# Third pass over the edges of a four-layer graph network: gathered rows as three bf16 parts

## The chip, the cores and the metric

The kernel runs on one core of one Trainium2 chip. The metric is the device time of one execution in microseconds (us). The five engines are TensorE (PE; its weight loads are listed apart as PEld), VectorE (DVE), ScalarE (ACT), GpSimd (POOL) and SyncE (SP).

## What is computed

A graph of 6250 nodes with 128 features each and 200000 edges, sorted by destination, goes through four layers. The third is a plain graph convolution:

```python
h = relu(layernorm(x))
h = feat * (out_deg ** (-0.5))[:, None]
agg = jax.ops.segment_sum(h[src], dst, num_segments=n)   # fp32
rst = relu((agg @ weight) * (in_deg ** (-0.5))[:, None] + bias)
x = x + rst
```

The other three layers are attention layers over the same edges. All is fp32.

## The kernel before

Nodes stand in 49 tiles of 128. Edges stand in 391 groups of 512 (4 tiles of 128 edges); a group whose edges reach over a border of node tiles is visited once for each node tile, so there are 440 visits, in the order that the destinations give. Each layer is a phase that writes a table of rows to DRAM and a pass over the edges that gathers from it. The passes run one after another; every phase ends in a barrier of all engines.

In the third pass (`conv_pass`, 5771 to 8032 us of the span):

- GpSimd runs `fetch`: for each of 392 groups four indirect DMAs (L465, 1568 in all) bring 128 rows each of the table `conv_rows` into one of 14 slots. A row has 129 fp32 numbers, 516 B: 128 features and a 1, which counts the in-degree. Before it fills a slot again it waits (L463) until TensorE's visits of the group that was there are done (`sum_done`). In its other three passes `fetch` puts a small tensor operation (L472, the pause) behind each gather; in this pass it does not.
- VectorE makes, 8 visits ahead, the one-hots of a visit (`pick`, L1033): 4 matrices of 128 edges by 128 nodes, written as fp32.
- TensorE multiplies them with the gathered rows, 4 matmuls of 129 columns a visit that add into one of 8 PSUM banks (L1022). It reads slot and due group of four visits at a time from a table (L411, L386), and waits for the group's rows, the one-hots and the bank. The trace shows each fp32 matmul as two weight loads and two matmuls.
- VectorE adds the bank to the node tile's sums in SBUF (L1042), after the add before it is done.

The loops are rolled: 32 visits are written out, then 16 visits an iteration. ScalarE has no work in this pass.

In the phase ahead (`conv_inputs`, l2pre, 5608 to 5771 us) ScalarE writes the finished rows (L1825) in 7 sets of 7 node tiles into two buffers, and SyncE stores each set to DRAM (L1741). GpSimd works on the set's inputs (L1753 to L1758), clears the sums (L1761) and has nothing after.

## Time and profile before

| | us |
|---|---|
| median of 3 runs | 10693.53 (10691.29 to 10695.21) |
| profiled execution, its own time | 10696.8 |
| its span, first to last instruction | 10695.1 |
| gathers of pass 1, first to last issue | 535.7 to 2938.3 |
| pass 2 | 3116.2 to 5567.7 |
| pass 3 | 5776.9 to 8021.0 |
| pass 4 | 8184.6 to 10578.7 |

A row of a group of instructions gives line, engine, operation, output and inputs, the count, then busy time, mean ns of one, and the idle time of the engine just before them by what ended it. Where a wait's releaser is inferred, "issue" means that the profile shows nothing that the engine waited for. A timeline row gives start, duration and, in brackets, the idle time before.

### The profile page before, as it was taken

Reading aid. Unit: us, or ns where it says so; the run is one execution under the profiler, and the core shown is the slowest. Engines: PE = TensorE matmul, PEld = TensorE weight load, DVE = VectorE, ACT = ScalarE, POOL = GpSimd, SP = SyncE. Lnnn points to the kernel's source line nnn. Section 1 sums busy time; section 2 is a strip of 40 time slices with the busy share of each in tenths; the row PEclk is TensorE's granted clock in tenths of the full one; section 3 lists DMA queues with packets and bytes.
Section 4 is the critical chain, followed back from the end, with each engine's and each line's share of the span. In section 5 each row is a group of like instructions: output and inputs, shape, how many; then the busy total and the mean of one; then the engine's idle time right before and its main releaser. Section 6 shows DMA issues by size and latency. Waiting matters only on the chain. (4 is left out here: it accounts for less than half of the span.)

```text
span 10695.1 us, 165052 instructions
## 1 busy us (share of the span) xinstructions
PE 6694.1 (63%) x38290; PEld 5319.6 (50%) x38291; DVE 5218.1 (49%) x13802; ACT 2509.1 (23%) x6808; POOL 7984.3 (75%) x11114
## 2 busy tenths in 40 slices
PE   4977777777756667666663333333337777777776
PEld 3656665655535555555553232232224555555554
DVE  4266666666665555555553111111114555555555
ACT  1333333333343333333333000000002111111111
POOL 0188888888848888888865666666663888888884
PEclk9966666676765555555556555565556666666667
DMA  3333333333312212222111222222222332333332
GB/s 112 148 88 88 87 87 87 87 88 88 87 46 47 46 44 46 45 46 45 44 40 46 46 46 46 47 46 46 46 46 63 87 87 87 87 87 87 87 87 63
DMA packets 379652, 731.26 MB, mean 68 GB/s; under 512 B 169770, under 2 KB 219233, under 8 KB 373126
## 3 DMA queue, kind: packets, MB, share of 16 engines
q0 software_dynamic: 251264, 621.88, 22.1%
q1 hardware_dynamic: 100762, 97.56, 2.8%
q10 hardware_dynamic: 27500, 10.39, 0.4%
q8 instruction: 48, 0.79, 0.0%
q14 instruction: 78, 0.64, 0.0%
HBM read 652.50 MB, written 76.88 MB: 68 GB/s over the span
## 5 line engine op out<-in xcount | busy, mean ns | idle before, releaser
L465 POOL DMA_INDIRECT edges_rows<-conv_rows,edges_idx_r x1568 | 1536.9, 980 | 773.6 <-issue 457.9
L465 POOL DMA_INDIRECT edges_rows<-gat_rows,edges_idx_r x1568 | 1562.8, 997 | 336.1 <-issue 260.1
L465 POOL DMA_INDIRECT edges_rows<-kv_typed,edges_idx_r x1568 | 1597.6, 1019 | 267.6 <-issue 263.5
L465 POOL DMA_INDIRECT edges_rows<-kv_rows,edges_idx_r x1568 | 1522.2, 971 | 271.6 <-issue 267.7
L1022 PE MATMUL edges_ps_sum<-edges_rows,edges_pick 128*128 x3520 | 763.3, 355 | 1511.7 <-issue 1386.9
L629 PE MATMUL edges_ps_sum<-edges_wv,edges_pick 128*128 128x132 f32 x7040 | 1671.9, 409 | 20.9 <-issue 13.4
L472 POOL TENSOR_TENSOR edges_pause<-edges_pause 128x56 f32<-128x56 f32 x4704 | 1599.9, 340 | 108.1 <-issue 18.1
L629 PEld LDWEIGHTS edges_ps_sum<-edges_wv,edges_pick 128*128 128x128 f32 x7040 | 1427.0, 297 | 256.6 <-issue 246.5
L1022 PEld LDWEIGHTS edges_ps_sum<-edges_rows,edges_pick 128*128 128x128 f32 x3520 | 647.9, 257 | 1627.1 <-issue 1625.7
L1120 PE MATMUL edges_ps_q<-q,edges_pick_t 128*128 x3520 | 748.7, 379 | 674.5 <-DVE edges_prod L1184 649.7
L1042 DVE TENSOR_TENSOR sums<-sums,edges_ps_sum 128x129 f32 x440 | 126.9, 288 | 1858.5 <-DMA edges_rows<-gat_rows,edges_idx_r 1486.5
L1120 PEld LDWEIGHTS edges_ps_q<-q,edges_pick_t 128*128 128x128 f32 x3520 | 645.4, 274 | 779.2 <-issue 779.0
L1110 PE MATMUL edges_ps_sum<-edges_wv,edges_pick 128*128 128x136 f32 x3520 | 814.0, 400 | 7.4 <-DVE sums L1206 7.4
L1110 PEld LDWEIGHTS edges_ps_sum<-edges_wv,edges_pick 128*128 128x128 f32 x3520 | 697.6, 286 | 166.1 <-issue 161.3
L611 PE MATMUL edges_ps_q<-q,edges_pick_t 128*128 x3520 | 750.1, 378 | 36.7 <-issue 15.2
L611 PEld LDWEIGHTS edges_ps_q<-q,edges_pick_t 128*128 128x128 f32 x3520 | 655.9, 277 | 66.5 <-issue 60.3
L815 DVE TENSOR_TENSOR edges_wv<-edges_rows,edges_wv 128x512 f32<-128x512 f32 x880 | 636.0, 723 | 3.8 <-issue 3.0
L1151 ACT ACTIVATE edges_wv<-edges_gap 128x32 f32<-128x32 f32 x440 | 113.1, 257 | 2075.7 <-DVE edges_gap L1213 1857.8
L1184 DVE TENSOR_TENSOR edges_prod<-edges_rows,edges_ps_q 128x512 f32<-128x512 f32 x440 | 301.5, 685 | 585.1 <-POOLq L475 306.5
L915 DVE TENSOR_TENSOR edges_lo_hot<-iota_bf,edges_src_lo 128x512 bf16<-128x512 bf16 x440 | 314.3, 714 | 558.7 <-remote 425.7
L1174 DVE TENSOR_TENSOR edges_pick<-edges_ps_iota,edges_local 128x512 f32<-128x512 f32 x440 | 304.3, 692 | 543.1 <-issue 530.0
L772 DVE TENSOR_TENSOR x<-iota_bf,edges_local 128x512 bf16<-128x512 bf16 x440 | 314.8, 715 | 473.4 <-issue 385.4
(345 smaller groups left out, 10934.8 us busy)
## 6 DMA issues: line engine op xcount, KB each, us to landing
kv_typed<-l0pre_out SPq DMA_DIRECT2D x49, 1024.0 KB
edges_rows<-kv_typed,edges_idx_r POOLq DMA_INDIRECT x1568
edges_rows<-gat_rows,edges_idx_r POOLq DMA_INDIRECT x1568
edges_rows<-conv_rows,edges_idx_r POOLq DMA_INDIRECT x1568
edges_rows<-kv_rows,edges_idx_r POOLq DMA_INDIRECT x1568
edges_feat_r<-visit_features ACTq DMA_DIRECT2D x660, 10.0 KB
kv_rows<-l3pre_kv SPq DMA_DIRECT2D x7, 896.0 KB
edges_flag_r<-visit_flags ACTq DMA_DIRECT2D x220, 16.0 KB
```

Of the source, the lines that this page charges most:

```text
L465: pool.indirect_dma_start(rows[:, k, g * width:(g + 1) * width], None, table, bass.IndirectOffsetOnAxis(ap=idx_r[:, k, g:g + 1], axis=0)). ...
L472: nc.gpsimd.tensor_tensor(pause, pause, pause, ALU.add).then_inc(paused, 1)
L611: mm = nc.tensor.matmul(ps_q[s % 2][:, g * D:(g + 1) * D], pick_t[:, s % 2, g * P:(g + 1) * P], q[:, bass.ds(b * D, D)], start=True, stop= ...
L629: mm = nc.tensor.matmul(ps_sum[s % 2][:, 0:aw], pick[:, s % 2, g * P:(g + 1) * P], wv[:, s % 3, g, :], start=g == 0, stop=g == G - 1)
L772: nc.vector.tensor_tensor(pick_b[:, s, :].rearrange("p (g n) -> p g n", g=G), c["iota_bf"].unsqueeze(1).broadcast_to([P, G, P]), bcast(loc ...
L815: nc.vector.tensor_tensor(wv4[:, s % 3, :, :, 0:hd], vals, bcast(wv4[:, s % 3, :, :, hd], [P, G, heads, hd]), ALU.mult).then_inc(wv_done, 1)
L915: ins = nc.vector.tensor_tensor(hot[:, s % 2], c["iota_bf"][:, 0:n].unsqueeze(1).broadcast_to([P, G, n]), bcast(digits[:, bass.ds(u * G, G ...
L1022: mm = nc.tensor.matmul(ps_sum[k % banks][:, 0:aw], pick[:, k % deep, g * P:(g + 1) * P], now[:, g, :], start=g == 0, stop=g == G - 1)
L1110: mm = nc.tensor.matmul(ps_sum[s % 2][:, 0:aw], pick[:, s % 6, g * P:(g + 1) * P], wv[:, s % 3, g, :], start=g == 0, stop=g == G - 1)
L1120: mm = nc.tensor.matmul(ps_q[s % 2][:, g * D:(g + 1) * D], pick_t[:, s % 2, g * P:(g + 1) * P], q[:, bass.ds(b * D, D)], start=True, stop= ...
L1174: nc.vector.tensor_tensor(pick[:, s % 6, :].rearrange("p (g n) -> p g n", g=G), ps_iota[:, 0:P].unsqueeze(1).broadcast_to([P, G, P]), bcas ...
L1184: nc.vector.tensor_tensor(prod[:].rearrange("p (g d) -> p g d", g=G), of_slot(rows, slot, width)[:, :, 0:D], ps_q[s % 2][:].rearrange("p ( ...
```

## The change

The table `conv_rows` holds for each feature three bf16 numbers whose sum is the fp32 number exactly: the high part, the high part of the rest, and what is left. A row is 385 bf16 numbers (770 B): 128 high, 128 mid, 128 low parts and the 1. GpSimd makes the parts in `conv_inputs`: four operations a set, each behind the one before by a semaphore. The one-hots are written as bf16, TensorE does one matmul of 385 columns a tile, and VectorE adds mid, low with the count, and high in three operations, each behind the one before.

```diff
+PARTS = 3 * D + 1
@@ conv_pass
-        rows = p.sb("rows", [P, SLOTS, G * aw])
+        rows = p.sb("rows", [P, SLOTS, G * PARTS], BF16)
-        pick, local = p.sb("pick", [P, deep, GE]), ...
+        pick, local = p.sb("pick", [P, deep, GE], BF16), ...
-                        mm = nc.tensor.matmul(ps_sum[k % banks][:, 0:aw], pick[:, k % deep, g * P:(g + 1) * P], now[:, g, :],
+                        mm = nc.tensor.matmul(ps_sum[k % banks][:, 0:PARTS], pick[:, k % deep, g * P:(g + 1) * P], now[:, g, :],
-                    nc.vector.tensor_tensor(blk, blk, ps_sum[k % banks][:, 0:aw], ALU.add).then_inc(acc_done, 1)
+                    nc.vector.tensor_tensor(blk[:, 0:D], blk[:, 0:D], ps_sum[k % banks][:, D:2 * D], ALU.add).then_inc(mid_done, 1)
+                    dve.wait_ge(mid_done, u + 1)
+                    nc.vector.tensor_tensor(blk, blk, ps_sum[k % banks][:, 2 * D:PARTS], ALU.add).then_inc(low_done, 1)
+                    dve.wait_ge(low_done, u + 1)
+                    nc.vector.tensor_tensor(blk[:, 0:D], blk[:, 0:D], ps_sum[k % banks][:, 0:D], ALU.add).then_inc(acc_done, 1)
@@ conv_inputs
-        table = p.sb("table", [P, 2, CH, D + 1])
+        table, rest_rows = p.sb("table", [P, 2, CH, D]), p.sb("rest_rows", [P, CH, D])
+        parts = p.sb("parts", [P, 2, CH, PARTS], BF16)
@@ SyncE
-                    sp.wait_ge(row_done, (k + 1) * CH)
-                    sp.dma_start(dram["conv"][...], table[:, k % 2]).then_inc(stored[k % 2], 16)
+                    sp.wait_ge(low_cut, k + 1)
+                    sp.dma_start(dram["conv"][...], parts[:, k % 2]).then_inc(stored[k % 2], 16)
@@ GpSimd
+                pool.wait_ge(framed, 1)
+                for k in range(SETS):
+                    row = table[:, k % 2]
+                    high, mid, low = (parts[:, k % 2, :, n * D:(n + 1) * D] for n in range(3))
+                    pool.wait_ge(row_done, (k + 1) * CH)
+                    if k >= 2:
+                        pool.wait_ge(stored[k % 2], 16 * (k // 2))
+                    if k:
+                        pool.wait_ge(low_cut, k)
+                    nc.gpsimd.tensor_copy(high, row).then_inc(high_cut, 1)
+                    pool.wait_ge(high_cut, k + 1)
+                    nc.gpsimd.tensor_tensor(rest_rows[:], row, high, ALU.subtract).then_inc(high_off, 1)
+                    pool.wait_ge(high_off, k + 1)
+                    nc.gpsimd.tensor_copy(mid, rest_rows[:]).then_inc(mid_cut, 1)
+                    pool.wait_ge(mid_cut, k + 1)
+                    nc.gpsimd.tensor_tensor(low, rest_rows[:], mid, ALU.subtract).then_inc(low_cut, 1)
@@ ScalarE
-                        act.wait_ge(stored[t // CH % 2], 16 * (t // CH // 2))
+                        act.wait_ge(low_cut, t // CH - 1)
@@ VectorE
-                nc.vector.memset(table[:], 1.0).then_inc(framed, 1)
+                nc.vector.memset(parts[:], 1.0).then_inc(framed, 1)
```

On VectorE a visit of the third pass reads as follows before the change (`edges_pick` are the one-hots, `sums` the node tiles' sums, TENSOR_LOAD the read of the node tile's number):

```order
L1042 TENSOR_TENSOR sums<-sums,edges_ps_sum 128x129
L1033 TENSOR_TENSOR edges_pick<-iota_bf,edges_local 128x512
L377 TENSOR_LOAD seat_rows
L1042 ISA
L1042 TENSOR_TENSOR sums<-sums,edges_ps_sum 128x129
```

and with it, where two adds more stand between two makings of one-hots:

```order
L1048 TENSOR_TENSOR sums<-sums,edges_ps_sum 128x128
L1035 TENSOR_TENSOR edges_pick<-iota_bf,edges_local 128x512
L378 TENSOR_LOAD seat_rows
L1044 ISA
L1044 TENSOR_TENSOR sums<-sums,edges_ps_sum 128x128
L1046 TENSOR_TENSOR sums<-sums,edges_ps_sum 128x129
L1048 TENSOR_TENSOR sums<-sums,edges_ps_sum 128x128
```

On TensorE the visit has the same instructions in the program, only the matmul's shape differs. Before:

```order
L1022 ISA
L1022 MATMUL edges_ps_sum<-edges_rows,edges_pick 128x129
L1022 ISA
L1022 MATMUL edges_ps_sum<-edges_rows,edges_pick 128x129
```

With the change:

```order
L1024 ISA
L1024 MATMUL edges_ps_sum<-edges_rows,edges_pick 128x385
L1024 ISA
L1024 MATMUL edges_ps_sum<-edges_rows,edges_pick 128x385
```

On GpSimd the phase ahead ended with the clearing of the sums; behind it now stand, seven times, the four operations of a set:

```order
L1768 MEMSET sums 128x924 x7
L1778 CAST l2pre_parts<-l2pre_table 128x7x128
L1780 TENSOR_TENSOR l2pre_rest_rows<-l2pre_table,l2pre_parts 128x896
L1782 CAST l2pre_parts<-l2pre_rest_rows 128x7x128
L1784 TENSOR_TENSOR l2pre_parts<-l2pre_rest_rows,l2pre_parts 128x7x128
```

## Rows read from the trace of the kernel before

**Rows 1.** The page: busy time, share of the span and instructions, each engine.

```profile
PE 6694.1 (63%) x38290; PEld 5319.6 (50%) x38291; DVE 5218.1 (49%) x13802; ACT 2509.1 (23%) x6808; POOL 7984.3 (75%) x11114
```

**Rows 2.** Windows: the third and the fourth pass; columns in the heading row.

```profile
core 0: us, PE busy (x) PEld busy (x) DVE busy (x) ACT busy (x) POOL busy (x), PEclk, DMA share, GB/s
5800.00:8000.00 2200.00, 736.90 (x3384) 624.17 (x3384) 371.23 (x839) 0.00 (x0) 1507.36 (x1539) 0.58 0.21 47
8250.00:10500.00 2250.00, 1621.06 (x7028) 1296.78 (x7029) 1200.68 (x2481) 303.55 (x826) 1964.12 (x2944) 0.65 0.30 87
```

**Rows 3.** Line L465, third and fourth pass: duration ns min/median/max, first and last start.

```profile
L465 POOL DMA_INDIRECT edges_rows<-conv_rows,edges_idx_r x1568: 938/944/1462, 5776.9 to 8021.0; - x196
L465 POOL DMA_INDIRECT edges_rows<-kv_rows,edges_idx_r x1568: 951/960/1480, 8184.6 to 10578.7; - x196
```

**Rows 4.** Groups of the third pass: busy, mean | idle before, releasers.

```profile
L465 POOL DMA_INDIRECT edges_rows<-conv_rows,edges_idx_r x1568 | 1536.9, 980 | 773.6 <-issue 457.9 <-DMA edges_rows<-gat_rows,edges_idx_r 170.8 <-PE edges_ps_sum L1022 72.4
L1022 PEld LDWEIGHTS edges_ps_sum<-edges_rows,edges_pick 128*128 128x128 f32 x3520 | 647.9, 257 | 1627.1 <-issue 1625.7
L1033 DVE TENSOR_TENSOR edges_pick<-iota_bf,edges_local 128x512 f32<-128x512 bf16 x440 | 302.3, 689 | 22.8 <-DMA edges_local<-visit_locals 14.7 <-issue 7.4 <-PE edges_ps_sum L1022 0.7
L1042 DVE TENSOR_TENSOR sums<-sums,edges_ps_sum 128x129 f32 x440 | 126.9, 288 | 1858.5 <-DMA edges_rows<-gat_rows,edges_idx_r 1486.5 <-issue 194.1 <-PE edges_ps_sum L1022 174.9
```

**Rows 5.** GpSimd's timeline about a wait: start, duration, idle before.

```profile
6510.23 0.94 POOL L465 DMA_INDIRECT edges_rows<-conv_rows,edges_idx_r  x1 [0.30 <-issue]
6511.48 0.94 POOL L465 DMA_INDIRECT edges_rows<-conv_rows,edges_idx_r  x1 [0.31 <-issue]
6520.50 1.10 POOL L465 DMA_INDIRECT edges_rows<-conv_rows,edges_idx_r  x1 [8.08 <-DMA edges_rows<-gat_rows,edges_idx_r]
```

**Rows 6.** Timeline of PE matmuls around the same wait.

```profile
6501.52 0.38 PE L1022 MATMUL edges_ps_sum<-edges_rows,edges_pick 128*128 x1 [2.44 <-issue]
6519.73 2.51 PE L1022 MATMUL edges_ps_sum<-edges_rows,edges_pick 128*128 x10 [0.35 <-issue]
```

**Rows 7.** Windows about that wait: slow, fast, slow; and an earlier slow one.

```profile
6463.00:6519.00 56.00, 11.97 (x50) 9.14 (x50) 2.82 (x6) 0.00 (x0) 37.53 (x40) 0.57 0.22 49
6519.00:6543.00 24.00, 17.84 (x107) 16.04 (x106) 12.61 (x28) 0.00 (x0) 17.62 (x17) 0.79 0.19 42
6543.00:6605.00 62.00, 10.25 (x27) 7.53 (x28) 2.76 (x6) 0.00 (x0) 41.31 (x44) 0.53 0.22 48
5909.00:5957.00 48.00, 9.26 (x26) 6.90 (x26) 2.67 (x6) 0.00 (x0) 36.01 (x39) 0.52 0.23 52
```

**Rows 8.** Line L386, register work of PE's sequencer: duration min/median/max.

```profile
L386 PEldq FUSED_REGOPS  x440: 2/151/1396, 5773.7 to 8025.6; - x147
```

**Rows 9.** DMA queues that moved anything between 6000 and 7900 us: packets, MB, share.

```profile
q0 software_dynamic: 42401, 87.60, 20.6%
q1 hardware_dynamic: 6768, 0.68, 0.3%
```

**Rows 10.** Groups of GpSimd in the phase ahead (l2pre).

```profile
L1758 POOL TENSOR_TENSOR x<-x,l2pre_rows 128x896 f32<-128x896 f32 x7 | 17.0, 2435 | 0.0
L1757 POOL TENSOR_TENSOR h<-h,l2pre_selves 128x896 f32<-128x896 f32 x7 | 13.4, 1919 | 1.0
L1761 POOL MEMSET sums<- 128x924 f32 x7 | 5.8, 864 | 25.2 <-DVE q L1856 25.2
```

**Rows 11.** The phase's end: stores as issued, and their time to landing.

```profile
5758.55 7.72 SPq L1741 DMA_DIRECT2D conv_rows<-l2pre_table  x3
DMA to landing us min/median/max: 4.2/4.6/5.0
```

**Rows 12.** VectorE's L1856 with GpSimd at work, then with it idle.

```profile
L1856 DVE TENSOR_TENSOR q<-sums,h 128x896 f32<-128x896 f32 x5 | 14.3, 2856 | 11.2 <-POOL h L1757 11.1
L1856 DVE TENSOR_TENSOR q<-sums,h 128x896 f32<-128x896 f32 x2 | 2.2, 1091 | 0.1
```

**Rows 13.** VectorE's memset at the start of the phase ahead.

```profile
5610.33 1.56 DVE L1837 MEMSET l2pre_table<- 128x1806 f32 x1 [0.32 <-issue]
```

21 lines of the change are left out of this document (10 added, 11 removed).

## Prediction, written before the changed kernel ran

> **What bounds the kernel now.** I read the page's engine line first. GpSimd is busy for 75% of the span and TensorE for 63% [rows 1], but a share over four passes says nothing on one of them, so windows by pass come next. In the third pass GpSimd is busy 1507 of 2200 us, TensorE 737, VectorE 371, ScalarE not at all, and the DMA engines 0.21 [rows 2]. Only GpSimd can set the pace there. The gathers' own line gives it: 1568 of them, the first issued at 5776.9 and the last at 8021.0, so 2244 us for 1567 steps [rows 3]. Undisturbed, one follows another in 1.25 us, 0.94 busy and 0.30 between [rows 5]; 1567 x 1.248 = 1956 us. The mean gather is 980 ns against a median of 944 [rows 3, 4], which over 1568 is 57 us. That leaves 2244 - 1956 - 57 = 231 us, and the group row shows them: GpSimd was idle 170.8 us put down to a DMA and 72.4 us put down to L1022 [rows 4]. The first releaser can't be right, since it names gathers of the table `gat_rows`, which were over 200 us before this pass; what GpSimd waits for there is `sum_done`, a slot that TensorE holds. So **231 us of waiting for TensorE is all that faster matmuls can win in the pass**; the other 2013 us are the issue of gathers, and the change leaves their number alone.
>
> Why does an engine that is busy a third of the time hold up another? The timelines show it. At 6501.52 one matmul stands alone after 2.44 us of idle; at 6519.73 ten follow in 2.51 us [rows 6]. TensorE works in **fast bursts and slow stretches**. In the burst from 6519 to 6543 it made 106 weight loads (8 a visit, so 13.3 visits) in 24 us; in the next 62 us, 28, which is 3.5 visits or 17.7 us each; in an earlier slow stretch 26 in 48 us, 14.8 us a visit. The 56 us ahead of the burst begin with the end of another burst and have 50 [rows 7]. In slow stretches it isn't the matmuls: register work of TensorE's sequencer, which takes 151 ns as the median, takes up to 1396 [rows 8]. The whole instruction stream crawls. GpSimd gathers on at full pace through it (44 x 0.94 = 41 of 62 us, rows 7), fills the 14 slots, and has to stop; at its wait before 6520.50 [rows 5] TensorE recovers. A gather every 1.25 us without a gap is what the other passes don't have: in the fourth, with its pause, a gather takes (10578.7 - 8184.6) / 1567 = 1.53 us [rows 3], and TensorE does 7028 matmuls in 2250 us without slow stretches [rows 2]. I take it that the uninterrupted issue of gathers causes the slow stretches and that GpSimd's waits end them.
>
> **The change, part by part.** *TensorE.* A visit now issues 4 weight loads and 4 matmuls where the trace has 8 and 8. In a burst this matters little. In a slow stretch each load and each matmul costs a step of its own, so a visit should take about half: 17.7 -> 8.9 us, bounds 7.4 (half of 14.8) and 11.2 (half of a whole visit at the crawl of one load or matmul each 1.4 us, the 1396 ns of rows 8: 16 x 1.4 = 22.4).
> Now the cycle. A visit uses 392/440 = 0.89 of a group, and GpSimd makes one in 5.0 us, 0.20 a us. After a burst the slots fill at 0.20 - 0.89/17.7 = 0.15 a us. In the cycle from 6519 the slow stretch has 53 us of gathering and 9 of waiting (62 - 44 x 1.25 is 7, and short gaps), so it fills 53 x 0.15 = 8 slots. With 8.9 us a visit they fill at 0.20 - 0.10 = 0.10 a us and take 80 us. Gathering per cycle goes from 24 + 53 = 77 us to 24 + 80 = 104, and the waits, once a cycle, from 231 us to 231 x 77/104 = 171: **-60 us**. With 11.2 us a visit it is -34, with 7.4 it is -86.
> *Gathers.* 770 B instead of 516 B. A gather of 1024 B rows in the fourth pass has a median of 960 ns against 944 [rows 3], so 0 to 1568 x 0.016 = +25 us. I take 0, since the 16 ns may as well come from the pause behind it. Three halves of the bytes put the DMA share from 0.21 to 0.31, and the fourth pass lives with 0.30 [rows 2].
> *VectorE.* One-hots stay 689 ns, an add is 288 [rows 4]; a visit goes from 0.98 to 0.69 + 3 x 0.29 = 1.56 us, in all 440 x 1.56 = 686 us of 2244, with waits between the chained adds some 750. TensorE's next use of a bank waits for the last add, 8 visits later. In a burst of 24 us VectorE still does 14 to 15 visits against the 13.3 that TensorE did. So it costs nothing, but it is the next bound of a burst. If VectorE's work is what lengthens gathers from 944 to 980 ns, that term grows with it, 57 x 1.56/0.98 = 91: at most +34 us. I take 0: the one-hots read and write SBUF alone and don't grow, the adds read PSUM.
> *The phase ahead.* Each set gets four operations of 896 elements on GpSimd. For the two subtractions the rows are 1.92 to 2.44 us, for the two copies I have only a memset of 0.86 below and these same 1.92 above [rows 10]; I take 1.5 for a copy, near the middle, so 2 x 2.0 + 2 x 1.5 = 7.0 us a set, bounds 5.6 and 9.8. The first four sets are 15 us apart and hide it. The last three stores were issued at 5758.55 and until 5766.27 [rows 11]: there sets 4 to 6 are complete, and GpSimd takes 3 x 7.0 = 21 us from 5758.5, to 5779.5. A store lands 4.6 us after its issue [rows 11]; with 1.5 times the bytes 4.6 to 6.9, I take 5.3. End at 5784.8 instead of 5765.9 + 4.6 = 5770.5: **+14 us**, bounds +9 (5.6, 4.6) and +24 (9.8, 6.9). VectorE's memset grows from 1806 to 5390 elements, by 1.56 x 2 = 3.1 us [rows 13], ahead of the shares that GpSimd waits for. GpSimd waits there for loads from DRAM too, which hide part of it: +1 us, bounds 0 and 3.
> VectorE's operations of 896 elements take 2856 ns with GpSimd at work and 1091 with it idle [rows 12], so the parts will also lengthen VectorE's work in this phase; most of that is done before the first set is ready, and I add nothing. The Trainium skill speaks against the change here (SBUF — State Buffer, "Who interferes with whom"): an operation of VectorE with two SBUF inputs contends with a GpSimd instruction that reads SBUF. By that rule L1856 has to take longer beside GpSimd, and the trace agrees. Of the copies the Trainium skill says (GPSIMD Engine Reference, 3.1) some 1.8 cycles an element with one input; by the Trainium skill's figure, as an estimate, 896 elements take 1.34 us, and the sum for the phase would be +13 instead of +14.
>
> **Sum.** -60 + 14 + 1 = -45 us against the profiled execution's own 10696.8: 10652. The median of the runs is 3.3 lower, so 10649.
>
> **Rivals.** *A, the slow stretches go.* If it takes TensorE's own rate of instructions to bring them on, half of it may stay below. For it: the other passes have none. Against it: they have more matmuls a us than this one [rows 2], so the rate alone isn't the cause. All 231 us less would be -231 + 15 = -216, 10478; a partial case lies between.
> *B, nothing is won in the stretches*, because their pace hangs on something that the change doesn't halve: the program has as many instructions for TensorE as before. Then +15 (with gathers at +25, +40): 10709. The Trainium skill (Runtime: NRT & Kernel Launch, "Instruction fetch mechanics") has a taken branch outside the resident pages wait for a fetch by DMA. By that rule the crawl would be TensorE fetching its loop; but between 6000 and 7900 us only the queues of the gathers and of SyncE's lists moved anything [rows 9], so the trace doesn't bear it out.
> *C, slower: waits too short to end a stretch.* A stretch ended where GpSimd stood 8.08 us [rows 5]. With the slots full it stands only until the next visit frees one. At 17.7 us a visit that is 17.7/0.89 - 5.0 = 15 us at most, and the stretch ends first. At 8.9 us it is 5 us, and if a stretch needs more than that, TensorE goes on crawling and GpSimd loses 5 us on each group until a wait happens to be long enough. With two such waits a cycle (104 us of gathering) beside the one of 8 us, the pass has 18/104 x 2013 = 348 us of waits, 117 more than now; with one, 13/104, 252, 21 more. I price the rival between, +70 + 15 = +85: 10778. It decides where the waits of a cycle come to more than 231 x 104/2013 = 12 us; up to there the pass is no slower than before.
>
> **Chances.** Forecast (stretches stay, visits in them take half) 0.42; A 0.20; B 0.15; C 0.23. A measurement of this kernel can tell about 0.2%, 21 us, from no change. The forecast, from -86 to +25 about its -45, gives 0.34 faster and 0.08 the same; A is faster; B is 0.10 the same and 0.05 slower; C is slower. Faster 0.54, same 0.18, slower 0.28. The likeliest case alone reaches from 10605 to 10690. The range has to take in most of A and C: 10480 to 10785, which leaves out the far side of C (+117 with dearer gathers) and a win larger than all waits.
>
> **What would show it.** In the changed kernel's third pass: the gathers' pitch in a burst is still 1.25 us, their median 944 to 960 ns; weight loads come to 1760; in slow stretches a visit takes 7 to 11 us, and the cycle is longer, some 110 instead of 86 us. GpSimd's idle time beside "issue" falls from 250 us to about 190 (forecast), to near nothing (A), stays (B), or rises with many waits of 3 to 6 us (C). The pass begins about 15 us later after the phase ahead. Wrong would be: gathers that take longer by themselves, VectorE as the releaser of TensorE over the whole pass, or four operations of GpSimd that take over 10 us a set.

## The result, and the profile after

The changed kernel is slower. Its median over 13 runs is 10720.68 us (10705.17 to 10743.90), that of the kernel before, run beside it 13 times, 10695.21 us (10681.24 to 10721.04); the ratio is 1.0024, interval 1.0014 to 1.0034. I had forecast 10649 us, 72 less, and faster; size and sign were wrong, though the time lies in the range. The profiled execution spans 10709.5 us against 10695.1.

The page of the changed kernel, the busy line and then the groups of the third pass; columns as in [rows 1] and [rows 4]:

```profile
PE 6519.6 (61%) x36530; PEld 4863.4 (45%) x36531; DVE 5469.6 (51%) x14682; ACT 2510.5 (23%) x6808; POOL 8050.0 (75%) x11142
...
L466 POOL DMA_INDIRECT edges_rows<-conv_rows,edges_idx_r x1568 | 1535.4, 979 | 736.3 <-issue 474.3
...
L1024 PE MATMUL edges_ps_sum<-edges_rows,edges_pick 128*128 x1760 | 607.8, 448 | 1691.5 <-issue 1530.5
...
L1024 PEld LDWEIGHTS edges_ps_sum<-edges_rows,edges_pick 128*128 128x128 bf16 x1760 | 198.5, 113 | 2100.6 <-issue 2074.7
...
L1044 DVE TENSOR_TENSOR sums<-sums,edges_ps_sum 128x128 f32 x440 | 126.0, 286 | 1590.2 <-PE edges_ps_sum L1024 585.1
```

The change did what it says: 1760 loads of 113 ns where there were 3520 of 257 [rows 4]. GpSimd's idle time beside "issue" is 736.3 - 474.3 = 262 us where it was 316. That is a fall of about the size that the forecast gave as a sign, but no win in the pass: 65.5 of the 316 us stand before the first gather and 10.4 of the 262, because GpSimd now works on the parts in that time. Without them 250 us became 252. The gathers by themselves, and the whole pass as a window (the columns of [rows 2]):

```profile
L466 POOL DMA_INDIRECT edges_rows<-conv_rows,edges_idx_r x1568: 942/949/1466, 5773.3 to 8033.5; - x196
```

```profile
core 0: us, PE busy (x) PEld busy (x) DVE busy (x) ACT busy (x) POOL busy (x), PEclk, DMA share, GB/s
5773.30:8033.50 2260.20, 600.50 (x1728) 194.85 (x1728) 628.88 (x1724) 0.00 (x0) 1534.30 (x1568) 0.56 0.27 69
```

First to last gather is 2260.2 us; it was 2244.1 [rows 3]. Where the 14.4 us between the two spans come from: the phase ahead began 16 us earlier in the changed kernel (5592.9 against 5608.8), before any changed instruction (22.6 us behind the last gather of pass 2, where it was 41.1); from there to the first gather of the third pass it lost 12.3 us; in the pass 16.1; behind it 1.9. Without the chance gain at the end of pass 2 that is +30, near the medians' +25.5.

The phase ahead, by the four new operations of GpSimd and the store (duration ns min/median/max, first and last start):

```profile
L1778 POOL CAST l2pre_parts<-l2pre_table x7: 935/936/1502, 5697.7 to 5757.1; 128x896 bf16<-128x896 f32 x7
L1780 POOL TENSOR_TENSOR l2pre_rest_rows<-l2pre_table,l2pre_parts x7: 1817/1826/1841, 5699.3 to 5758.2; 128x896 f32<-128x896 f32 x7
L1782 POOL CAST l2pre_parts<-l2pre_rest_rows x7: 935/937/960, 5701.1 to 5760.0; 128x896 bf16<-128x896 f32 x7
L1784 POOL TENSOR_TENSOR l2pre_parts<-l2pre_rest_rows,l2pre_parts x7: 1818/1827/1844, 5702.2 to 5761.1; 128x896 bf16<-128x896 f32 x7
L1748 SPq DMA_DIRECT2D conv_rows<-l2pre_parts x7: 359/359/360, 5704.0 to 5762.9; - x7
L1858 DVE MEMSET l2pre_parts<- x1: 4550/4550/4550, 5595.1 to 5595.1; 128x5390 bf16 x1
```

A set takes 0.94 + 1.83 + 0.94 + 1.83 = 5.5 us, 5.9 with the gaps.

**The third pass, visit by visit.** VectorE's last add of each visit marks its end, and the time from one to the next sorts the visits: over 5 us, in a slow stretch; the others, in a burst or on the way into one. Waits of GpSimd are the times over 1 us from the end of one gather to the start of the next; waits whose starts are less than 14 us apart make one cluster. Worked out from all 440 visits and 1568 gathers:

| third pass | before | after |
|---|---|---|
| first to last gather | 2244.1 | 2260.2 |
| slow visits | 120, mean 14.7 us | 173, mean 10.1 us |
| all slow visits together | 1765 us | 1752 us |
| other visits | 319, mean 1.50 us | 266, mean 1.93 us |
| waits over 1 us | 44, in all 240 us | 49, in all 261 us |
| clusters | 38 of 6.3 us | 30 of 8.7 us |
| waits in a cluster | 1.2 | 1.6 |

Slow visits did get cheaper, and clusters rarer. But more visits had to be made slowly, the kernel spent the same 1750 us in slow stretches, and each cluster cost more: 30 x 8.7 = 261 against 38 x 6.3 = 240. (Clusters and their means are rounded; the sums are the measured ones. The split into number and price hangs on the 14 us: with 10 us it is 38 of 6.3 against 33 of 7.9, with 20 us 33 of 7.3 against 29 of 9.0. The price rises in each.)

The same loss read by visits: those over 5 us come to 13 us less in all, the others to 512 us instead of 480. There are 53 fewer of these, but a typical one is longer: their median is 1.52 us where it was 0.95.

A cluster in the changed kernel, in GpSimd's timeline (start, duration, idle before):

```profile
6712.15 0.94 POOL L466 DMA_INDIRECT edges_rows<-conv_rows,edges_idx_r  x1 [1.59 <-issue]
...
6725.45 0.94 POOL L466 DMA_INDIRECT edges_rows<-conv_rows,edges_idx_r  x1 [3.60 <-issue]
6729.85 0.94 POOL L466 DMA_INDIRECT edges_rows<-conv_rows,edges_idx_r  x1 [3.45 <-issue]
...
6735.94 0.94 POOL L466 DMA_INDIRECT edges_rows<-conv_rows,edges_idx_r  x1 [2.65 <-issue]
...
6742.94 0.95 POOL L466 DMA_INDIRECT edges_rows<-conv_rows,edges_idx_r  x1 [2.29 <-issue]
...
6753.91 0.94 POOL L466 DMA_INDIRECT edges_rows<-conv_rows,edges_idx_r  x1 [6.26 <-PE edges_ps_sum L1024]
```

and TensorE's timeline at its end:

```profile
6751.65 4.14 PE L1024 MATMUL edges_ps_sum<-edges_rows,edges_pick 128*128 x16 [17.99 <-issue]
6757.76 4.48 PE L1024 MATMUL edges_ps_sum<-edges_rows,edges_pick 128*128 x16 [1.97 <-DVE sums L1048]
```

Five waits of 1.6 to 3.6 us pass by and no burst follows; then one of 6.3 us, and 16 matmuls come in 4.14 us. In the kernel before, the wait at the same kind of place was one piece of 8.08 us [rows 5].

**What a slow visit is made of.** TensorE's timeline inside a slow stretch of the changed kernel:

```profile
6796.97 0.10 PEld L1024 LDWEIGHTS edges_ps_sum<-edges_rows,edges_pick 128*128 128x128 bf16 x1 [1.99 <-issue]
6798.36 0.10 PEld L1024 LDWEIGHTS edges_ps_sum<-edges_rows,edges_pick 128*128 128x128 bf16 x1 [1.30 <-issue]
...
6803.97 0.10 PEld L1024 LDWEIGHTS edges_ps_sum<-edges_rows,edges_pick 128*128 128x128 bf16 x1 [4.73 <-issue]
6805.36 0.10 PEld L1024 LDWEIGHTS edges_ps_sum<-edges_rows,edges_pick 128*128 128x128 bf16 x1 [1.30 <-issue]
6806.77 0.10 PEld L1024 LDWEIGHTS edges_ps_sum<-edges_rows,edges_pick 128*128 128x128 bf16 x1 [1.30 <-issue]
6808.16 0.10 PEld L1024 LDWEIGHTS edges_ps_sum<-edges_rows,edges_pick 128*128 128x128 bf16 x1 [1.29 <-issue]
```

Most loads start 1.40 us apart, though each takes 0.10: between them stands an instruction of the sequencer (a wait, or the slot's address) that shows some 700 ns, where in a burst it takes some 50 or less. The change halved the loads and matmuls; the waits and address computations of a visit, and the table read with its register work at every fourth, stayed. They now carry the steps: 1209 register and wait instructions of TensorE's sequencer take 0.7 or 1.4 us in this pass (between 0.65 and 0.75 us or twice that, the table reads left out), 366 in the kernel before.

### The profile page after: what moved, and what is told of

It is laid out like the page before. It is cut to its first block and busy times, and to the rows that moved or that the text cites. A ratio compares the mean times of both kernels' runs of the same rounds, so it can differ in the third digit from the quotient of the medians.

```text
span 10709.5 us, 162446 instructions
## 1 busy us (share of the span) xinstructions
PE 6519.6 (61%) x36530; PEld 4863.4 (45%) x36531; DVE 5469.6 (51%) x14682; ACT 2510.5 (23%) x6808; POOL 8050.0 (75%) x11142
## 5 line engine op out<-in xcount | busy, mean ns | idle before, releaser
L466 POOL DMA_INDIRECT edges_rows<-conv_rows,edges_idx_r x1568 | 1535.4, 979 | 736.3 <-issue 474.3
L473 POOL TENSOR_TENSOR edges_pause<-edges_pause 128x56 f32<-128x56 f32 x4704 | 1609.0, 342 | 106.9 <-issue 16.4
L1024 PE MATMUL edges_ps_sum<-edges_rows,edges_pick 128*128 x1760 | 607.8, 448 | 1691.5 <-issue 1530.5
L1024 PEld LDWEIGHTS edges_ps_sum<-edges_rows,edges_pick 128*128 128x128 bf16 x1760 | 198.5, 113 | 2100.6 <-issue 2074.7
L1044 DVE TENSOR_TENSOR sums<-sums,edges_ps_sum 128x128 f32 x440 | 126.0, 286 | 1590.2 <-PE edges_ps_sum L1024 585.1
```

What stands on the lines that cost most here:

```text
L466: pool.indirect_dma_start(rows[:, k, g * width:(g + 1) * width], None, table, bass.IndirectOffsetOnAxis(ap=idx_r[:, k, g:g + 1], axis=0)). ...
L473: nc.gpsimd.tensor_tensor(pause, pause, pause, ALU.add).then_inc(paused, 1)
L1024: mm = nc.tensor.matmul(ps_sum[k % banks][:, 0:PARTS], pick[:, k % deep, g * P:(g + 1) * P], now[:, g, :], start=g == 0, stop=g == G - 1)
```

## Two kinds of sitting

One fact has to come ahead of the experiments, since it decides what each could show. The slow stretches are there at some times and not at others, with the same program. The runs fell into sittings, each on one chip as far as the record names it:

| sitting | kernel before, us | slow stretches in the third pass |
|---|---|---|
| the result above | 10695 | yes |
| b_pause4, b_pause1, a_pause1, a_still | 10683 | yes |
| a_split, a_oneadd, b_wide, b_pause2 | 11028 | yes, and passes 1 and 2 longer |
| b_again, a_hold, b_hold, a_narrow | 10294 | no |
| a_again, a_hold_2, a_narrow_2 | 10301 | no |
| a_hold_3; a_hold_4 | 10299; 10300 | no |
| a_hold_oneadd | 10293 | no |

The second sitting and those of a_hold_3 and a_hold_4 were on one and the same chip, so it isn't a property of the chip; nor of the kernel. What switches it I don't know. Kernels are compared within a sitting only.

## Experiments

**A pause behind each gather (b_pause4).** The kernel before, with the call as the other passes have it:

```diff
+        pause, paused = p.sb("pause", [P, 56]), p.sem("paused")
-                fetch(nc, pool, ..., sum_done, slot_free, None, None)
+                fetch(nc, pool, ..., sum_done, slot_free, pause[:], paused)
```

> The kernel before, with GpSimd's small pause operation (56 elements, some 0.28 us) behind each gather of the third pass, as the other three passes have it. Theory G (gathers issued without a gap bring on TensorE's slow stretches): the stretches and the waits for sum_done go, each gather comes 1.53 us after the last as in the fourth pass, 1567 x 1.53 = 2400 us instead of 2244, the run some 150 us longer, at 10845. Rival (the stretches come from something in the third pass itself, its 3280-odd matmuls and loads or its lists): the stretches stay, TensorE's register operations still go up to 1.4 us, and the waits of about 230 us come on top of the longer pitch or part of them; the run over 10900.

It ran in 10847.06 us, the kernel before in 10683.09. The waits over 1 us are 4, together 8.7 us, and register work of TensorE's sequencer never takes long:

```profile
L386 PEldq FUSED_REGOPS  x440: 146/148/175, 5777.2 to 8158.7; - x147
```

against a longest of 1396 in [rows 8]. First to last gather is 2393.9 us, forecast 2400. So a gap behind each gather takes the stretches of the third pass away, and costs more than they do.

**One pause in four gathers (b_pause1, a_pause1), and two (b_pause2).** `fetch` gets a list of the gathers that have a pause behind them:

```diff
-            if pause is not None:
-                pool.wait_ge(paused, j * G + (g + 1))
+            if pause is not None and g in at:
+                pool.wait_ge(paused, j * len(at) + (at.index(g) + 1))
```

> The kernel before, with one such pause in each group of four gathers of the third pass. Theory G, if one gap in four is enough: no slow stretches, a group in 4 x 1.25 + 0.3 = 5.3 us, 392 x 5.3 = 2078 us plus up to 57 for long gathers, so the pass 110 to 165 us shorter and the run at 10530 to 10590. If one gap in four is not enough: stretches and waits as before (230 us) and up to 110 us of pauses on top, of which the waits absorb a part; the run at 10700 to 10800. Rival (the stretches have nothing to do with gaps): the same second figure.

> The changed kernel, with one such pause in each group of four gathers of the third pass. Theory G: the stretches go here too, and then before and after differ only by the phase ahead: about 12 us above the kernel before with the same pause. Rival (the changed kernel's loss in the pass is VectorE's three adds or the wider rows, not the stretches): it stays 17 us or more above the other in the pass alone, besides the 12 of the phase ahead, some 30 us above it in all.

> The kernel before with the pause behind the second and the fourth gather of each group. With one a group a group takes 5.16 us where it runs free, and the slow stretches stay; with four, 6.12 us and there are none. With two the free pace is some 5.35 us, 392 x 5.35 = 2097 us plus about 60 for long gathers, 2157 against 2244. If two gaps end the stretches, the run is at 10610. If they don't, waits of 100 us or more come on top: 10700 or later.

b_pause1 took 10679.67 us (before: 10683.09), and neither figure was right. The stretches stay, but the waits fall from 240 to 174 us (a pause that stands inside a wait is counted in; 158 us without), and the pauses use up what that gives: 2246.9 us from first to last gather. With two pauses the waits are 118 us (105 without), the pass 2281.3, the run 11053.26 against 11028.19. Each gap shortens the waits and costs as much or more; none of the three numbers of gaps wins.

a_pause1 took 10702.82 us, 23 above b_pause1. Its pass is not longer but 9 us shorter (2238.1); the phase ahead with the waits around it is 16 longer, and the rest came before and behind, where nothing was changed. Both kernels still have stretches, and their waits are equal, 174 and 175 us. So the loss in the third pass is no fixed price of the changed instructions. That speaks against adds and rows as the cause, but with one profile of each it is not shown.

A look into a stretch of b_pause1 shows the same steps on TensorE (loads; here a load and a matmul alternate):

```profile
6725.66 0.29 PEld L1023 LDWEIGHTS edges_ps_sum<-edges_rows,edges_pick 128*128 128x128 f32 x1 [1.81 <-issue]
6728.46 0.29 PEld L1023 LDWEIGHTS edges_ps_sum<-edges_rows,edges_pick 128*128 128x128 f32 x1 [2.51 <-issue]
6731.26 0.29 PEld L1023 LDWEIGHTS edges_ps_sum<-edges_rows,edges_pick 128*128 128x128 f32 x1 [2.51 <-issue]
6734.06 0.29 PEld L1023 LDWEIGHTS edges_ps_sum<-edges_rows,edges_pick 128*128 128x128 f32 x1 [2.51 <-issue]
```

2.80 us from load to load, 1.40 for each load and each matmul. Eight and eight make 22.4 us, the longest visit that the kernel before has, and has 18 times.

**No slot addresses on TensorE (a_still).** The changed kernel, matmuls on a tile of zeros:

```diff
+        still, still_set = p.sb("still", [P, G, PARTS], BF16), p.sem("still_set")
-                    now = of_slot(rows, slot, PARTS)
+                    now = still[:]
```

> The changed kernel, with TensorE's matmuls of the third pass reading a tile of zeros that stays in place, so that no address of a slot is computed: four register operations fewer of TensorE's sequencer a visit. The sums leave out the gathered rows. Theory S (in a slow stretch a visit of the changed kernel costs its sequencer's six instructions, 6 x 1.4 = 8.4 us, and 21.7 for each fourth with the list to read): a visit falls to 2 x 1.4 = 2.8 us, or what its 8 loads and matmuls need at their own step of 0.7 or 1.4 us (5.6 to 11.2), and 16 to 19 for each fourth; three visits and one come to 33 to 45 instead of 46.9, and the waits fall from 261 us to below 200, the run to about 10650. Rival (the loads and matmuls set a visit in the stretches): 8.4 us stays for three visits of four, and the waits stay within 20 us of 261.

10704.44 us; waits 211 us, slow visits 8.7 us on average (10.1 in the changed kernel), the pass 2215.6. Waits and visits fell as theory S has it, the waits by 50 us where it wanted over 61. The run gained little against the changed kernel's first profile because its pass 2 and the way into the phase ahead took 33 us more, where nothing was changed. The timeline shows what held up the rest. VectorE:

```profile
6672.31 0.29 DVE L1050 TENSOR_TENSOR sums<-sums,edges_ps_sum 128x128 f32 x1
6673.77 0.69 DVE L1037 TENSOR_TENSOR edges_pick<-iota_bf,edges_local 128x512 bf16<-128x512 bf16 x1 [1.17 <-issue]
6680.77 0.29 DVE L1046 TENSOR_TENSOR sums<-sums,edges_ps_sum 128x128 f32 x1 [6.31 <-issue]
...
6683.58 0.75 DVE L1037 TENSOR_TENSOR edges_pick<-iota_bf,edges_local 128x512 bf16<-128x512 bf16 x1 [1.88 <-issue]
```

Now VectorE crawls. It waits for nobody ("issue", 6.31 us) while its sequencer does the waits and the block address of one visit in steps of 1.4 us; 592 of its register and wait instructions in this pass show 0.7 or 1.4 us, in the changed kernel 41, in the kernel before 1. TensorE's own fell from 1209 to 205, and it waits for VectorE. So the crawl is not bound to TensorE. Why it moved to VectorE here, no run shows.

**Loads and matmuls back to eight (a_split).** The changed kernel, each matmul cut in two:

```diff
-                    for g in range(G):
-                        mm = nc.tensor.matmul(ps_sum[k % banks][:, 0:PARTS], pick[...], now[:, g, :], ...)
+                    for lo, hi in ((0, 193), (193, PARTS)):
+                        for g in range(G):
+                            mm = nc.tensor.matmul(ps_sum[k % banks][:, lo:hi], pick[...], now[:, g, lo:hi], ...)
```

> The changed kernel with each matmul of 385 columns cut into two, of 193 and 192 columns, each with its own weight load: 8 loads and 8 matmuls a visit again, as in the kernel before, all else as changed. The time between VectorE's last adds shows visits of over 5 us (slow ones) with a mean of 14.7 us in the kernel before and 10.1 in the changed one; the others take 1.5 and 1.9 us. Theory N (in a slow stretch a visit costs TensorE's instructions, however many of them are loads and matmuls): slow visits go back to 14 to 15 us, fast ones stay at 1.9, so the slots fill sooner and the waits rise from 261 us to 320 or more; the run at 10770 or later. Rival (the number of loads and matmuls doesn't set a slow visit): mean 10 us, the run at 10705 to 10720.

11185.92 us where the kernel before had 11028.19. Of the whole time much is outside the third pass (within this sitting pass 1 varies by 56 us and pass 2 by 36), so the pass itself has to be read: 2295.9 us, waits 319 us in 83 pieces, slow visits 12.3 us. Theory N expected 320 us or more, and 14 to 15 us a visit. In the same sitting the pass took 2271.1 us in a_oneadd (waits 291 us) and 2264.6 in b_wide. Against a_oneadd, which also has two adds less, the pass is 25 us longer; but b_wide has eight loads and matmuls too, and its pass is 6 us shorter than a_oneadd's. So what halving loads and matmuls is worth in the pass is not shown; a profile of the changed kernel itself in this sitting is lacking.

**One add (a_oneadd).** The changed kernel with

```diff
-                    nc.vector.tensor_tensor(blk[:, 0:D], blk[:, 0:D], ps_sum[k % banks][:, D:2 * D], ALU.add).then_inc(mid_done, 1)
...
-                    nc.vector.tensor_tensor(blk[:, 0:D], blk[:, 0:D], ps_sum[k % banks][:, 0:D], ALU.add).then_inc(acc_done, 1)
```

> The changed kernel with VectorE's first and third add left out; only the low part and the count are added, so two of the three parts are missing in the sums. VectorE's visit falls from 1.56 to 0.98 us. Theory V (the three adds make the bursts poor, 1.9 us for each fast visit instead of 1.5, so that only 266 visits instead of 319 are fast ones): fast visits go back to 1.5 us or less, 320 or more of 440 are fast, slow ones stay at 10 us, and the waits fall from 261 to 150 us or less; the run at 10600 or earlier. Rival C (waits are too short to end a stretch, whatever VectorE does): fast visits get shorter, but the waits stay over 230 us and the run over 10680.

11119.03 us against 11028.19. Theory V wanted waits of 150 us or less and falls: they are 290.7. The mean of the fast visits stays at 1.92 us, since more of them lie between 3 and 5 us (53 instead of 37); their median fell from 1.52 to 1.29. With the adds gone, the next limit in a burst is TensorE: 75 visits took 1.2 to 1.4 us, four matmuls of 385 columns at 0.32 us each, where the kernel before made 147 visits in 0.8 to 1.0 us.

**Wider rows (b_wide).** The kernel before with `WIDTH = 193` in place of 129 for the slots, the gathers and the table; matmuls read `now[:, g, 0:aw]`.

> The kernel before with conv rows of 193 fp32 words (772 bytes, where it had 516 and the changed kernel 770); the matmuls still read 129 columns. Theory W (wider rows matter): gathers take 949 ns or more as the median instead of 944, and the pass is the 17 us longer that the changed kernel showed, the run some 15 to 25 us above the kernel before, with the larger stores. Rival, which I hold: median 944 to 950 ns, 0 to +8 us in the pass, up to 5 us in the phase ahead for stores of half again the bytes.

11085.66 us against 11028.19, which a single run of each in this sitting can't read. The gather's median is 946 ns (944 in [rows 3]), so 1568 x 2 = 3 us: that part of the expectation holds. Waits are 261 us and the pass 2264.6, with no profile of the kernel before beside it. The slow visits are 14.5 us (14.7 in the kernel before, in another sitting); rows that are wider hardly change them. Whether they lengthen the waits stays open.

**Holding GpSimd for several slots at once (a_hold, b_hold).** If a stretch ends only after GpSimd stood long enough in one piece, fewer and longer waits should cost less:

```diff
+HOLDS = {1: 0, 2: 1, 3: 2, 4: 3, 5: 4, 6: 6}
-        elif k % HALF == HALF - 1 and known(j + 1, SLOTS):
-            pool.wait_ge(used, at_least_one(pool, visits[HALF - 1], NV))
-        elif known(j, SLOTS):
-            pool.wait_ge(used, at_least_one(pool, visits[k % HALF - 1], NV))
+        elif k % HALF in holds and known(j + holds[k % HALF] - (k % HALF - 1), SLOTS):
+            pool.wait_ge(used, at_least_one(pool, visits[holds[k % HALF]], NV))
```

with `{1: 3, 5: 6}` in the third pass. Beside them the kernel before as it is (b_again), and one add with 129 columns (a_narrow):

```diff
-                        mm = nc.tensor.matmul(ps_sum[k % banks][:, 0:PARTS], pick[...], now[:, g, :],
+                        mm = nc.tensor.matmul(ps_sum[k % banks][:, 2 * D:PARTS], pick[...], now[:, g, 2 * D:PARTS],
```

> The kernel before, unchanged, profiled once more beside the others. By the first profile of it: 44 waits over 1 us on GpSimd in the third pass, 240 us in all, in 38 clusters (waits less than 14 us apart) of 6.3 us; slow visits 14.7 us. How far this one differs is the noise of these readings: I expect 225 to 260 us and 34 to 42 clusters.

> The changed kernel, with GpSimd waiting for free slots twice in seven groups of the third pass, for four or three slots at once, instead of for one slot at six of seven groups; no wait is dropped, each comes earlier and covers those behind it. In the profile the changed kernel has 30 clusters of waits of 8.7 us in 1.6 pieces, the kernel before 38 of 6.3 us in 1.2 pieces. Theory C (a stretch ends only after GpSimd stood for some 6 us in one piece, and with cheaper slow visits the pieces got too short): clusters of one piece of 6 to 7 us again, some 30 of them, 180 to 210 us instead of 261; the run 50 to 80 us below the changed kernel, at 10640 to 10670 where the kernel before has 10690 (30 us or more below it). Rival (the sum of the waits ends a stretch, whole or in pieces, or waits are only the balance of a rate): 260 us of waits or more, the run no faster than the changed kernel, 25 us above the kernel before or more.

> The kernel before with the same two holds in seven groups. Theory C: its waits come in one piece already (1.2 a cluster), so little is won: 0 to 30 us less than 240 and, since slots are refilled later, perhaps as much back; the run within 20 us of the kernel before. Rival: as for the changed kernel with holds, the same change in both.

> The changed kernel with one add on VectorE and with matmuls of the low part and the count alone, 129 columns: the high and the mid part are missing in the sums. What is left of the change in the pass is half the loads and matmuls and the wider rows. The forecast's step (fewer instructions, longer cycles, the same wait in each): 30 clusters of 6.3 us, 170 to 190 us of waits, the pass 50 us shorter than that of the kernel before. Theory C: 30 clusters of 8 to 9 us in 1.5 pieces or more, 240 to 280 us, the pass as long as before or longer. Theory M (the 385 columns, 1.3 us a visit at the lower clock, make the bursts poor): waits below 200 us too, and in the run with one add and 385 columns not, which had 291.

This sitting had no stretches, so none of the four expectations was put to the test they were meant for (b_hold came within 20 us of the kernel before, as expected, but without waits). b_again:

```profile
span 10291.2 us, 165052 instructions
```

its gathers, second pass and third:

```profile
L465 POOL DMA_INDIRECT edges_rows<-gat_rows,edges_idx_r x1568: 952/958/2027, 3097.2 to 5457.1; - x196
L465 POOL DMA_INDIRECT edges_rows<-conv_rows,edges_idx_r x1568: 939/944/1460, 5645.7 to 7616.9; - x196
```

and the register work of TensorE's sequencer:

```profile
L386 PEldq FUSED_REGOPS  x440: 146/148/175, 5643.3 to 7602.9; - x147
```

The same program as in [rows 3] and [rows 8]: the pass takes 1971.2 us instead of 2244.1, with one wait of 1.1 us, and no register operation over 175 ns. 1567 x 1.248 = 1956, the undisturbed pace that the prediction worked out, is nearly all of it. The second pass is shorter too, 2359.9 us where the first profile has 2451.5.

So here one can read what the change costs without stretches. a_hold took 10321.04 us, b_hold 10296.33 (ratio to the kernel before 1.0003, interval 0.9993 to 1.0013), a_narrow 10310.12, the kernel before 10294.4. The holds do nothing where nothing waits, and the changed kernel with them is 27 us slower, ratio 1.0024 (1.0014 to 1.0034).

The changed kernel itself, the holds and the narrow matmuls came again in later sittings, none of which had stretches:

> The changed kernel, unchanged, profiled once more. On a chip with slow stretches (weight of evidence: passes with waits over 1 us on GpSimd, slow visits of 10 us): 240 to 290 us of waits in the third pass, in clusters of 8 to 9.5 us, 15 to 40 us above the kernel before. On a chip without them: no waits, the third pass 1977 us from first to last gather (6 above the kernel before), 14 to 15 us more between the passes, 20 to 28 us above the kernel before.

> The changed kernel with the two holds in seven groups, once more. On a chip with slow stretches, theory C (waits too short to end a stretch): clusters of one piece of 6 to 7 us, 180 to 210 us in all, 50 us or more less than the unchanged one beside it, and the run 30 us or more below the kernel before. Rival (the balance of rates sets the sum of the waits, in whatever pieces): within 20 us of the unchanged one in the sum, the run 15 to 40 us above the kernel before. On a chip without stretches it shows nothing, 27 us above the kernel before as it was.

> The changed kernel with one add and matmuls of 129 columns (the low part and the count alone; the high and the mid part are missing in the sums), once more. On a chip with stretches, theory C: as the changed kernel, clusters of 8 us or more in 1.5 pieces, 240 us or more in all. Theory M (columns and adds make the bursts poor): 170 to 190 us, clusters of 6.3 us, fast visits of 1.5 us where the changed kernel has 1.9, and the run at or below the kernel before. On a chip without stretches: 14 to 18 us above the kernel before, which is the phase ahead alone.

> The changed kernel with the two holds in seven groups, a third time, for a chip with slow stretches. Theory C (waits too short to end a stretch): 1.0 to 1.2 pieces a cluster, 6 to 7 us each, 180 to 210 us in all where the changed kernel had 261, the run at or below the kernel before. Rival (the balance of rates sets the sum, in whatever pieces): fewer and longer pieces, but 240 us or more in all, the run 15 us or more above the kernel before. On a chip without stretches: no waits, 25 us above the kernel before, and nothing told.

> The changed kernel with the two holds in seven groups, a fourth time, for a chip with slow stretches. Theory C: 1.0 to 1.2 pieces a cluster, 6 to 7 us each, 180 to 210 us in all where the changed kernel had 261. Rival (the balance of rates sets the sum): fewer and longer pieces, but 240 us or more in all. On a chip without stretches: no waits, 25 us above the kernel before, and nothing told.

a_again, the changed kernel, took 10328.27 us against 10300.57; a_hold_2 10325.28 (ratio 1.0023), a_narrow_2 10314.63 against the same; a_hold_3 10326.19 against 10298.97 (ratio 1.0025, interval 1.0015 to 1.0035); a_hold_4 10316.35 against 10299.52. The expectations for a sitting without stretches hold: 25 to 28 us more for the changed kernel (a_hold_4: 17), 14 to 16 for the one with one add and 129 columns. The gathers of a_again by duration, and as a group:

```profile
L466 POOL DMA_INDIRECT edges_rows<-conv_rows,edges_idx_r x1568: 940/946/1522, 5666.6 to 7646.0; - x196
```

```profile
L466 POOL DMA_INDIRECT edges_rows<-conv_rows,edges_idx_r x1568 | 1500.2, 957 | 491.1 <-issue 469.2 <-DMA edges_idx_r<-sources 10.9 <-DMA edges_rows<-conv_rows,edges_idx_r 7.6
```

The time from the last gather of pass 2 to the first of pass 3 is 205.0 us in a_again and 188.6 in b_again, +16.4; the pass 1979.4 and 1971.2 us, +8.2, which is the gathers' mean, 957 against 951 ns. The rest of the 35 us between these two profiles is spread over work that the change doesn't touch. They are of two sittings; within one, a_hold against b_hold, it is +14.2 and +6.9.

**One add with all columns (a_hold_oneadd).** Where no stretches are, a gather of the changed kernel still takes 6 ns more in the mean than before, and one with one add and 129 columns 1 to 2 ns more. To tell adds from columns, a_hold with the adds of a_oneadd:

> The changed kernel with the two holds in seven groups and with one add on VectorE (the high and the mid part are missing in the sums); the matmuls keep their 385 columns. Where no slow stretches occur (the holds did nothing there): if VectorE's two more adds lengthen the gathers, their mean is 952 ns and the pass 1972 to 1974 us from first to last gather; if the 385 columns do, 956 to 957 ns and 1977 us or more. Where stretches occur: by theory C (short waits don't end a stretch) clusters in 1.0 to 1.2 pieces of 6 to 7 us, 200 us in all; by the rival (balance of rates) 270 us or more.

Both figures were wrong: 10430.38 us against 10293.39, with no waits at all. Its gathers:

```profile
L465 POOL DMA_INDIRECT edges_rows<-conv_rows,edges_idx_r x1568 | 1612.1, 1028 | 488.7 <-issue 477.5 <-DMA edges_idx_r<-sources 10.1 <-PE edges_ps_sum L1023 0.6
```

Less work on VectorE, and the mean gather is 1028 ns instead of 957, while the median stays 946: some gathers are much longer. The fourth gather of a group takes 1261 ns in the mean, the other three 947 to 952. GpSimd's and VectorE's timelines side by side:

```profile
6507.38 0.94 POOL L465 DMA_INDIRECT edges_rows<-conv_rows,edges_idx_r  x1 [0.30 <-issue]
6508.63 1.39 POOL L465 DMA_INDIRECT edges_rows<-conv_rows,edges_idx_r  x1 [0.30 <-issue]
6510.32 0.95 POOL L465 DMA_INDIRECT edges_rows<-conv_rows,edges_idx_r  x1 [0.30 <-issue]
```

```profile
6508.28 0.29 DVE L1043 TENSOR_TENSOR sums<-sums,edges_ps_sum 128x129 f32 x1 [3.69 <-PE edges_ps_sum L1023]
6508.50 0.69 DVE L1034 TENSOR_TENSOR edges_pick<-iota_bf,edges_local 128x512 bf16<-128x512 bf16 x1
```

The one-hot runs from 8.50 to 9.19, and the gather that starts at 8.63, inside it, takes 1.39 us. In a_again, with three adds:

```profile
6507.46 0.95 POOL L466 DMA_INDIRECT edges_rows<-conv_rows,edges_idx_r  x1 [0.30 <-issue]
6508.71 0.95 POOL L466 DMA_INDIRECT edges_rows<-conv_rows,edges_idx_r  x1 [0.30 <-issue]
6509.96 0.95 POOL L466 DMA_INDIRECT edges_rows<-conv_rows,edges_idx_r  x1 [0.30 <-issue]
```

```profile
6509.05 0.29 DVE L1048 TENSOR_TENSOR sums<-sums,edges_ps_sum 128x128 f32 x1
6509.26 0.69 DVE L1035 TENSOR_TENSOR edges_pick<-iota_bf,edges_local 128x512 bf16<-128x512 bf16 x1
```

Here the one-hot starts at 9.26, inside a gather that started at 8.71, and it costs that gather nothing; it ends at 9.94, just ahead of the next one. The rule holds in all the profiles: every gather over 1.05 us in the third pass started while a one-hot ran; there are 183 in the kernel before with stretches and 36 without, 178 and 58 in the changed one, 378 in b_pause4, 352 here. What such a gather loses is what was left of the one-hot when it started, less some 0.13 us: in this run 87 gathers with 0.45 to 0.50 us left took 1.30 us in the mean, 35 with 0.15 to 0.20 left 0.98; in a_again those with less than 0.1 left took 0.945. The adds do nothing of the kind: 364 gathers of a_again started while an add ran, and took 945 ns in the mean. Over 945 ns each, the long ones come to 128 us here, 17 in a_again, 11 in b_again. So the question "adds or columns" had no answer of that form; what counts is where in the gathers' rhythm the one-hot falls. One add alone doesn't bring on the bad rhythm, for a_narrow has one add and 28 long gathers; whether it takes the 385 columns beside it, or the holds, no run shows. The Trainium skill (SBUF — State Buffer, "Who interferes with whom") has an operation of VectorE with two SBUF inputs contend with a GpSimd instruction that reads SBUF, and says that the order of issue decides which of the two blocks; the one-hot has two SBUF inputs, and the trace agrees with the order. By the same section a copy on VectorE was seen to stall DMAs and a `tensor_tensor` was not, for a reason that it calls inferred; the one-hot is a `tensor_tensor`, and here it held a gather up by 0.44 us (1.39 against 0.95).

## Why the prediction was wrong

**What bounds the kernel.** Right for the sittings with stretches: GpSimd's issue sets the pass, with 231 us of waits as all that could be won (240 as counted above). The cycle was read off one long example, 86 us with a wait of 9; the 38 clusters come once in 59 us in the mean, with 6.3 us each. Wrong by leaving out that the 231 us exist only at some times. In b_again they are 1 us, and there the change could not win anything.

**-60 us in the third pass: the step that failed.** It had three links.
*A slow visit takes half, 17.7 to 8.9 us.* It took 10.1 where it had been 14.7, a factor of 0.69. I let everything in a visit scale with loads and matmuls. TensorE's sequencer has instructions of its own in each visit and a table to read at every fourth; they step as slowly, and stayed (1209 steps of theirs where there had been 366; a_still, which took some away, brought 8.7). My upper bound of 11.2 would have been the better value, and gave -34.
*The cycle gets longer, so there are fewer waits.* Right in direction: 38 clusters became 30, a factor of 0.79; I had 77/104 = 0.74. At an unchanged 6.3 us that would be 30 x 6.3 = 189 us, 51 less than before, close to the -60.
*"and the waits, once a cycle".* This is what failed. I carried the wait of one cycle over unchanged. It rose from 6.3 to 8.7 us, 30 x 2.4 = 72 us, more than the longer cycles won. The sum of the two, -51 + 72 = +21, is the measured change of the waits, 240 to 261.

Why each got dearer fits rival C's mechanism: slow visits of 10 us free a slot after a few microseconds, GpSimd starts again, and the stretch goes on. Bursts do begin while GpSimd stands: 30 of 32 in the kernel before and 26 of 33 in the changed one (a burst: behind a slow visit the matmuls of three visits within 8 us), 5.5 and 5.3 us into the wait as the median. In the changed kernel 18 of 19 waits of 5.5 us or more were followed by four or more visits within 10 us, and 6 of 23 of those under 4.5 us; in the kernel before 21 of 24 and 10 of 16. That is an association, since a wait may also last because TensorE is late. Nor is there a fixed length that a wait must have: in a_split 45 of 56 waits under 4.5 us were followed by such visits, in a_still only 6 of 13 of those over 5.5 us.
A second explanation stands beside it, the one that a_narrow was to test: with 385 columns and three adds a burst empties fewer slots (a fast visit at 1.52 us as the median, not 0.95), so GpSimd is back at full slots sooner. By visits the loss is theirs: the time of the visits over 5 us hardly moved, 1765 to 1752 us here and 1688 to 1811 in all nine profiles with stretches, whatever was changed. Against it stands a_oneadd, with a median of 1.29 us and waits of 291 us, though in another sitting. The experiments that would have told the two apart are a_hold and a_narrow, and neither met a stretch. **So the wait's price is what failed; whether C's mechanism or the poorer bursts raised it stays open.** C's price was too high: I gave it 252 us of waits for one short wait a cycle and 348 for two, and took +70 between; what was measured is near the first, +21.

**VectorE, "it costs nothing".** Not settled. The fast visits went from 1.50 to 1.93 us, and 266 instead of 319 visits were fast; of these 188 took 1.4 to 1.7 us, the 1.56 that I had worked out as VectorE's need. But with one add (a_oneadd) the waits were no shorter, and the 385 columns are the next bound of a visit at 1.3 us. Neither bound was in my sum: I compared VectorE's 14 to 15 visits a burst with the 13.3 that TensorE had made, as if a burst always had 24 us.

**Gathers, 0 of 0 to +25.** The median rose by 2 to 5 ns, 3 to 8 us; the mean fell from 980 to 979 with stretches and rose from 951 to 957 without. Right in size. That it hangs on where the one-hot falls I had not seen, though rows of 1462 ns at most beside a median of 944 stood in [rows 3].

**The phase ahead, +15.** Right: 12.3 us in the first pair of profiles, 16.4 in the second, 14.2 in a_hold against b_hold. A set took 5.5 us against my 7.0 (a copy 0.94, not 1.5), which is the low bound; the memset 4.55 us, against my 1.56 + 3.1 = 4.7. The Trainium skill's figure for a copy (GPSIMD Engine Reference, 3.1), 1.34 us as an estimate, was too high as well; the trace has 0.94.

**The rivals.** A (stretches go) did not occur by the change. B (nothing is won in the stretches, 10709) came nearest in time: its reason, that something isn't halved, is the first link above. C (10778) named waits in several pieces, and the profile after has them, 1.6 a cluster instead of 1.2, at +70 us of waits where +21 came. The Trainium skill (Runtime: NRT & Kernel Launch, "Instruction fetch mechanics") has a taken branch outside the resident pages wait for a fetch. That this is the crawl stays unproved: the steps hit waits and register work anywhere in the loop, and the trace shows no queue but those of the gathers and of SyncE's lists; but what an engine waits for at a step no row shows.

## What to carry to other kernels

When a wait repeats in cycles, a change acts on two numbers, how often a cycle ends and what its end costs; work out both, and don't carry the second over because the first improves. Count every instruction of an engine that crawls, its waits and address computations too, before saying that half the matmuls is half the time. And profile the kernel before in a second sitting: here the 231 us that the change was after were gone in four of seven, while its cost of 25 to 28 us stayed in both where the changed kernel ran as it is.

## What was new about the hardware

- The same program on the same chip ran in 10683 us at one time and in 10299 at another. Two profiles of it from other sittings, [rows 3] and b_again, differ by 2244 against 1971 us in the third pass, and there the difference is the stretches in which the sequencers take 0.7 or 1.4 us an instruction.
- The second pass took 2452 us in the one and 2360 in the other, though it has a pause behind each gather. No register work of TensorE shows the steps there, but before the weight loads of L629 the longest idle time is 1.3 us in the one and 0.3 in the other, and GpSimd's waits come to 78 us instead of 8. What sets them is open. The lines (3116 to 5560 us; us in all, times, longest), first of the kernel before, then of b_again:

```profile
PEld edges_ps_sum L629 <- issue: 88.2, 424, 1.3
PEld edges_ps_sum L629 <- issue: 85.5, 433, 0.3
```

- In the third pass a gap behind each gather took the stretches away (b_pause4, in a sitting that had them), and each pause added shortens the waits: 240 us with none, 174 with one in four, 118 with two, 9 with four.
- In a stretch it is not always TensorE alone that crawls: in a_still VectorE did, and in b_pause1 register work and waits of GpSimd took 0.7 and 1.4 us (167 of them; 74 in the changed kernel, 1 in the kernel before).
- A gather that starts while VectorE compares two SBUF operands into SBUF ends later by what was left of the comparison, less some 0.13 us: up to 1.46 us in a_hold_oneadd instead of 0.95. One that started before it is not held up, and an add with one input from PSUM holds up none.
